# Global attention of a fused four-layer kernel: two query tiles per turn, V as the stationary operand, sums spread by a product

## Reference

```python
def _L2_conv_ref(x, cfc, theta_w, theta_b, phi_w, phi_b, g_w, g_b, out_w, out_b):
    ...
    gate = jax.nn.sigmoid(z)[:, :, None]
    s = xf * gate
    theta = jnp.einsum('oc,ncl->nol', theta_w, s) + theta_b[None, :, None]
    phi = jnp.einsum('oc,ncl->nol', phi_w, s) + phi_b[None, :, None]
    g = jnp.einsum('oc,ncl->nol', g_w, s) + g_b[None, :, None]
    attn = jax.nn.softmax(jnp.einsum('nci,ncj->nij', theta, phi), axis=-1)
    nl = jnp.einsum('ncj,nij->nci', g, attn)
    nl = jnp.einsum('oc,ncl->nol', out_w, nl) + out_b[None, :, None]
    out = s + nl
```

## Time and profile before

| | us |
|---|---|
| median of 3 runs (7589.86 to 7595.02) | 7592.06 |
| the profiled execution | 7591.81 |
| its span in the trace | 7590.1 |
| `softmax2` of batch 0, from the first copy of a query tile to the last write of `nl` | 1067.6 to 1517.2 |
| `softmax2` of batch 1 | 1576.5 to 2026.2 |

### The profile page before, as it was taken

How to read it: one execution, slowest core, us unless ns; L and a number is a source line. 1 busy time by engine, 2 the same in 40 slices (tenths; PEclk the granted TensorE clock), 3 DMA queues, 4 the chain that set the end, 5 groups by cost and what they waited for, 6 DMA issues and landing times. The chain is left out here.

```text
span 7590.1 us, 146447 instructions
## 1 busy us (share of the span) xinstructions
PE 6756.7 (89%) x42848; PEld 4634.2 (61%) x42848; DVE 6281.8 (83%) x9625; ACT 5783.1 (76%) x9094; POOL 5374.7 (71%) x3396
## 2 busy tenths in 40 slices
PE   6777889989779999999999999999999999999998
PEld 4656457767546666666666666666666666666666
DVE  4333754444459999999999999999999999999997
ACT  4454112222259999999999999999999999999997
POOL 3333000000049999999999999999999999999997
PEclk9988999999989999999999999999999999999998
DMA  2000000000010000000000000000000000000000
GB/s 71 20 22 22 1 1 0 0 0 0 10 52 10 1 1 1 1 1 2 10 1 1 1 1 1 2 27 1 1 1 1 1 2 2 4 4 4 4 4 6
DMA packets 75943, 56.06 MB, mean 7 GB/s; under 512 B 50776, under 2 KB 73464, under 8 KB 75032
## 3 DMA queue, kind: packets, MB, share of 16 engines
q1 hardware_dynamic: 72512, 53.88, 2.5%
q10 hardware_dynamic: 3288, 0.33, 0.0%
HBM read 37.80 MB, written 16.37 MB: 7 GB/s over the span
## 5 line engine op out<-in xcount | busy, mean ns | idle before, releaser
L1524 POOL TENSOR_TENSOR a_s<-a_s,a_v 128x784 f32<-128x784 f32 x1568 | 2912.8, 1858 | 321.6 <-ACT a_s L1735 305.7
L1560 PE MATMUL a_right_sides<-a_s,diag_d 128*128 128x392 f32 x6272 | 2294.0, 509 | 9.1 <-POOL a_s L1524 1.0
L1560 PEld LDWEIGHTS a_right_sides<-a_s,diag_d 128*128 128x128 f32 x6272 | 1136.7, 191 | 1057.5 <-POOL a_s L1524 306.7
L1656 DVE SCALAR_TENSOR_TENSOR a_kan<-a_s,spline_c,a_kan 128x784 f32<-128x784 f32 x1568 | 1622.9, 1035 | 51.6 <-issue 0.6
L1583 PEld LDWEIGHTS a_weighed<-a_V,a_probT 112*128 112x128 f32 x10976 | 1374.7, 193 | 162.2
L1517 POOL TENSOR_TENSOR a_inner<-a_inner,a_x 128x784 f32<-128x784 f32 x784 | 1458.6, 1860 | 0.0
L1583 PE MATMUL a_weighed<-a_V,a_probT 112*128 112x65 f32 x10976 | 1365.5, 270 | 0.0
L1735 ACT ACTIVATE a_s<-a_v 128x784 f32<-128x784 f32 x1568 | 1335.0, 852 | 4.7
L1726 ACT ACTIVATE a_v<-a_a 128x784 f32<-128x784 f32 x1568 | 1335.9, 852 | 0.3
L1572 PE MATMUL a_turned<-ident,a_prob 128*112 128x128 f32 x5488 | 856.7, 279 | 228.4 <-ACT a_probT L1742 226.6
L1627 DVE TENSOR_SCALAR a_x<-a_scores 128x392 f32<-128x392 f32 x1568 | 877.7, 560 | 20.1 <-PE a_scores L1547 20.1
(11 more groups left out here) (192 smaller groups left out, 6842.1 us busy)
## 6 DMA issues: line engine op xcount, KB each, us to landing
rows<-bias_rows_dram SPq DMA_DIRECT2D x112, 91.0 KB
X<-in_x_dram SPq DMA_DIRECT2D x4, 1568.0 KB, 13.7
a_q<-q_dram SPq DMA_DIRECT2D x392, 16.0 KB, 2.0
mask<-in_window_mask_dram SPq DMA_DIRECT2D x56, 98.0 KB
v_dram<-V SPq DMA_DIRECT2D x14, 227.5 KB, 2.3
a_V<-v_dram SPq DMA_DIRECT2D x4, 796.2 KB
q_dram<-Q SPq DMA_DIRECT2D x14, 224.0 KB, 1.9
k_dram<-K SPq DMA_DIRECT2D x14, 224.0 KB, 1.9
```

Of the source, the lines that this page charges most:

```text
L1524: eng.tensor_tensor(s, s, v, ALU.mult).then_inc(cubed, 1)
L1560: mm = eng.matmul(up[:, j, 0:SUB], steps[i][:, :], cubes[g][:, SUB * j:SUB * (j + 1)], start=(i == 0), stop=(i == 1))
L1656: eng.scalar_tensor_tensor(F, banked((s1, s2)[j][g][:, :]), c[:, 3 + j:4 + j], F, ALU.mult, ALU.add).then_inc(left_added, 1)
```

## The change

`softmax2` takes the queries in 14 pairs of tiles (`PAIR` = 224 queries, turn u) instead of 28 tiles. The scores of the two tiles (h = 0, 1) come one after the other, as eight groups. A chunk is now two key tiles of both query tiles, [112, 2, 224]: the same number of elements as before, 14 chunks per pair. In the products that weigh the values the operands change places: `gT` of a key tile is stationary, and the 224 turned columns move, so the output has channels on partitions and needs no turning. The division changes with it: DVE multiplies the identity by the inverse sums (`share`), PE multiplies that with a matrix of ones, which gives the inverse sums in every channel's row, and DVE copies them (`spread`) and multiplies the output with them into `nl` (`keep_spread`). ACT copies the even chunks and so the first of each pair, DVE the odd ones. ACT no longer places the output. The addition of `s` to the stream moves from DVE in `project_out2` to POOL in `project2`.

```diff
-                project2(nc, m, b, s, theta, phi, gT, gate_scale, gate_bias)
+                project2(nc, m, b, theta, phi, gT, gate_scale, gate_bias)
...
+            @block.gpsimd
+            def _(pool):
+                pool.wait_ge(gated, HALVES)
+                for f in range(HALVES):
+                    X = m.X[:, HALVES * b + f, :]
+                    pool.tensor_tensor(X, X, s[:, f, :], ALU.add).then_inc(with_s, 1)
+                pool.wait_ge(with_s, HALVES)
...
+        probT = [sb(f"probT{r}", [TILE, 2, PAIR]) for r in range(2)]
+        tp = [ps(f"turned{i}", [TILE, 2, 256]) for i in range(2)]
+        op = [ps(f"op{r}", [P, 2, 256]) for r in range(2)]
...
+        def copied(c, u):
+            return (copied_v if c % 2 else copied_a, 7 * (u + 1) + c // 2 + 1)
+
+        def copy_chunk(eng, copy, u, c, done):
+            eng.wait_ge(turned, 14 * u + c + 29)
+            eng.wait_ge(pv_done, 14 * u + c + 13)
+            copy(probT[c % 2][:, :, :], tp[c % 2][:, :, 0:PAIR]).then_inc(done, 1)
...
+                def values(eng, u, r):
+                    eng.wait_ge(exp_done, 2 * (u + 1))
+                    for c in range(TILES // 2 + 1):
+                        if c < TILES // 2:
+                            eng.wait_ge(*(copied(c - 2, u) if c >= 2 else copied(c + 12, u - 1)))
+                            for j in range(2):
+                                at = TILE * (2 * c + j)
+                                for h in range(2):
+                                    mm = eng.transpose(tp[c % 2][:, j, TILE * h:TILE * (h + 1)], prob[r][h][:, at:at + TILE], m.ident[0:TILE, 0:TILE])
                             mm.then_inc(turned, 1)
                         if c == 1:
-                            eng.wait_ge(o_normed, t + 1)
+                            eng.wait_ge(o_placed, u + 1)
                         if c >= 1:
-                            eng.wait_ge(*copied(c - 1, t))
-                            for j in range(4):
-                                k = 4 * (c - 1) + j
-                                mm = eng.matmul(op[:, :], probT[(r + c - 1) % 2][:, j, :], gT[:, k, :], start=(k == 0), stop=(k == TILES - 1))
+                            eng.wait_ge(*copied(c - 1, u))
+                            for j in range(2):
+                                k = 2 * (c - 1) + j
+                                mm = eng.matmul(op[r][:, 0, 0:PAIR], gT[:, k, :], probT[(c - 1) % 2][:, j, :], start=(k == 0), stop=(k == TILES - 1))
                             mm.then_inc(pv_done, 1)
...
+                def spread_shares(eng, u, r):
+                    eng.wait_ge(share_made, 2 * (u + 1))
+                    for h in range(2):
+                        mm = eng.matmul(op[r][:, 1, TILE * h:TILE * (h + 1)], ones[:, :], share[r][:, h, :], start=True, stop=True)
+                    mm.then_inc(shares_spread, 1)
...
-                pipeline(pe, TILES, [(scores, 0), (turn_out, 2), (values, 1)])
+                pipeline(pe, TURNS, [(scores, 0), (spread_shares, 2), (values, 1)])
...
-                pipeline(dve, TILES, [(row_max, 0), (normalise, 1)])
+                pipeline(dve, TURNS, [(row_max, 0), (keep_spread, 2), (normalise, 1)])
...
-                pipeline(act, TILES, [(copies, 1), (place_out, 2), (exponent, 0)])
+                pipeline(act, TURNS, [(copies, 1), (exponent, 0)])
...
-                for f in range(HALVES):
-                    X = m.X[:, HALVES * b + f, :]
-                    dve.tensor_tensor(X, X, s[:, f, :], ALU.add).then_inc(with_s, 1)
```

More of the change, by code:

```diff
@@ L1122, in copied @@
[L1122 to L1132, removed]
+        q = [sb(f"q{r}", [P, PAIR]) for r in range(2)]
@@ new lines, in softmax2 @@
+        prob = [[sb(f"prob{r}{h}", [TILE, L]) for h in range(2)] for r in range(2)]
+        probT = [sb(f"probT{r}", [TILE, 2, PAIR]) for r in range(2)]
+        share = [sb(f"share{r}", [TILE, 2, TILE]) for r in range(2)]
+        ones = sb("ones", [TILE, P])
+        spread = sb("spread", [P, PAIR])
+        gmax = [sb(f"gmax{r}", [TILE, 2, 4]) for r in range(2)]
+        rmax = [sb(f"rmax{r}", [TILE, 2]) for r in range(2)]
+        nmax = [sb(f"nmax{r}", [TILE, 2]) for r in range(2)]
+        rsum = [sb(f"rsum{r}", [TILE, 2]) for r in range(2)]
@@ L1142, in _ @@
+                pipeline(pool, TURNS, [(stage_q, 0)])
             @block.tensor
             def _(pe):
[L1144 to L1158, removed]
-                            for j in range(4):
-                                at = TILE * (4 * c + j)
-                                mm = eng.transpose(tp[(r + c) % 2][:, j, :], prob[r][:, at:at + TILE], m.ident[0:TILE, 0:TILE])
+                def scores(eng, u, r):
+                    eng.wait_ge(q_ready, u + 1)
+                    for h in range(2):
+                        for g in range(4):
+                            eng.wait_ge(s_copied, 8 * u + 4 * h + g + 1)
+                            for j in range(2):
+                                at = SUB2 * (2 * g + j)
+                                mm = eng.matmul(scp[g % 2][:, j, 0:SUB2], q[r][:, TILE * h:TILE * (h + 1)], phi[:, at:at + SUB2], start=True, stop=True)
+                            mm.then_inc(s_made, 1)
@@ L1183, in _ @@
+                pe.sem_inc(s_made, 16)
+                pe.sem_inc(turned, 28)
+                pe.sem_inc(pv_done, 14)
+                pe.wait_ge(ones_set, 1)
+                pipeline(pe, TURNS, [(scores, 0), (spread_shares, 2), (values, 1)])
             @block.vector
             def _(dve):
[L1185 to L1194, removed]
@@ L1208, in _ @@
-                pipeline(dve, TILES, [(row_max, 0), (normalise, 1)])
+                dve.sem_inc(copied_v, 7)
+                dve.sem_inc(o_placed, 2)
+                pipeline(dve, TURNS, [(row_max, 0), (keep_spread, 2), (normalise, 1)])
+                dve.wait_ge(o_placed, TURNS + 2)
             @block.scalar
             def _(act):
[L1212 to L1225, removed]
-                pipeline(act, TILES, [(copies, 1), (place_out, 2), (exponent, 0)])
-                act.wait_ge(o_placed, TILES + 1)
-def project_out2(nc, m, b, s, nl):
+                def copies(eng, u, r):
+                    for c in range(0, TILES // 2, 2):
+                        copy_chunk(eng, eng.copy, u, c, copied_a)
@@ new lines, in exponent, with project_out2 @@
+                def exponent(eng, u, r):
+                    for h in range(2):
+                        eng.wait_ge(max_ready, 2 * u + h + 1)
+                        eng.activation(prob[r][h][:, :], prob[r][h][:, :], ACT.Exp, bias=nmax[r][:, h:h + 1], accum_out=rsum[r][:, h:h + 1]).then_inc(exp_done, 1)
+                act.sem_inc(copied_a, 7)
+                pipeline(act, TURNS, [(copies, 1), (exponent, 0)])
+                act.wait_ge(exp_done, 2 * TURNS)
+def project_out2(nc, m, b, nl):
```

68 lines of the change are left out of this document (30 added, 38 removed).

## The result

The changed kernel takes 7478.99 us (median of four, 7471.93 to 7492.06) against 7590.96 (7589.22 to 7595.02): ratio 0.9858, interval 0.9845 to 0.987. A second comparison gave 7476.05 against 7587.33: 0.9851, 0.9836 to 0.9867.

What follows compares the result with a forecast made beforehand. PE and what makes it wait bound `softmax2`. Pairs gain 97.2 us, batch ends lose 9.6, `project_out2` gains 3.8: 91.4 off 7591.81 gives 7500.4, with the median 0.25 above, so 7501; range 7484 to 7541.

Steps and rivals of the forecast that it cites:

- Step 1: Weighing products in `softmax2`: 56 passes of 224 columns at 0.19 us replace 112 of 128, gaining 1.57 us per pair.
- Step 2: First copies of a pair: PE waits 0.58 us for chunk 0 and 0.35 for chunk 1, gaining 2.11 per pair.
- Step 3: Chunks between first and last: copies just fit behind PE's work, 1.145 us a chunk, cover 0.09, no further gain.
- copies bind: Rival on step 3's chunks: slower copies or handing over lengthen each chunk, 7512 to 7546, likely 7525; chance 0.17.
- Steps 4 to 6: Per pair: last copy gains 0.06 us, product with the ones loses 0.19, scores in eight groups lose 0.08.
- Step 7: Batch ends: PE waits 3.6 us for the last exponentials, then a lower clock; net loss 4.8 a batch, 9.6 altogether.
- Step 8: `project_out2` without DVE's additions ends one piece behind PE, at 13.2 us: gain 1.9 a batch, 3.8 in all.
- Step 9: POOL's additions in `project2`: 7.4 us for each half, 14.9 for both, hidden, costing nothing.
- the rest unnamed: Outcomes outside the forecast and named rivals, spread over both sides; no cause or size given.

## Why the prediction was wrong

It was right in the layer that it worked out, and wrong in what it left out.

- **The sum for the layer** was 91.4; the layer gave 96.8. A pair was to take 28.45 and took 28.23. `softmax2` gave 4.9 more than forecast and `project_out2` 1.4 more, while `project2` lost 0.8 in these traces.
- **Step 1**, the pass of 224 columns at 0.19: (1.156 - 0.385) / 4 = 0.193. Over 1568 passes that is 4 us less gain than forecast. That it is columns that count was shown with 256 of them. Width itself earns nothing: two tiles now move 224 columns per key tile and pass where they moved 2 x 128.
- **Step 2**, the first copies: right in mechanism, 1.24 instead of 1.35 for chunk 0 and a stand of 0.10 instead of 0.35 for chunk 1. From the copy's end to PE's product 0.05 passed, where I had 0.15, and DVE began the spread 1.08 after the transpose, not 1.23; the two instructions took 0.39 each (I had 0.43 and 0.40). This is worth 0.36 a pair more than forecast. The 0.15 went wrong by the operand and not by the engine. In the old order the copied tile is the stationary operand and has to be loaded after the copy: with ACT's copy too, the copy ends at 1284.73, the load starts at 1284.84, the product at 1284.87. In the new order the copied tile moves, and with DVE's copy first (1296.68 + 0.61) PE starts 0.07 behind it.
- **Step 3**: chunks held at 1.156; the thin cover was enough, and the rival "copies bind" did not come.
- **Steps 4 to 6**: 0.29 for the last copy (0.30 forecast), the product with the ones 0.43 (0.39 forecast), the scores 10.57 from their start to that product (1299.40 to 1309.97), which is 32 passes of 0.330 without a visible loss; the 10.74 in the row includes the last pass's own length.
- **Step 7**: PE waited 3.07 us beyond the product (3.6 forecast), then ran at half its clock as forecast, for 6.8 us in batch 0 and 3.4 in batch 1 (3.7 forecast).
- **Step 8**: 1.9 a batch was right for batch 1 (17.5 to 15.7). In batch 0 the clock stayed up, PE took 10.76 instead of 12.42, and the stage gained 3.4. The mechanism was named, but I took both batches alike. What keeps the clock up in one batch and not in the other, behind the same 2.53 us of rest, was not found.
- **Step 9**: POOL took 6.82 an addition (7.4 forecast) and stayed hidden: `project2` took 42.1 against 42.0.

**The step that failed** is none of the nine, but the sentence behind them: that the profiled execution goes to 7500.4 when the layer's sum is taken off, with all else unchanged. The sum put the change of the untouched last attention at nothing, without a reason; it measured 16.8. The kernel before has 16 to 17 us in that layer that most other kernels here don't have: of seven pauses tried on it one left 13 of them, and among the edits of the changed kernel the one with the addition on DVE has 20. 7501 less 16.8 is 7484, and 5 us more from the layer give 7479, the measured median. That it fits to the microsecond is partly luck, for the medians of the kernel before alone lie between 7587.3 and 7592.1 here. The layer's 5 us alone would have left the time at 7496, inside the range. The rivals did not hold this case either; "the rest unnamed" took its place. What remains open is why just these moments are bad. The trace shows what happens (PE's clock halves for 6.8 us in single blocks) and that two executions of one kernel repeat the layer's time to 0.1 us, though their first parts differ by 5 us. The blocks need not be the same ones: the first long one was the 81st in one execution of the kernel before and the 79th in the other. What in PE's work sets it off was not found.

## What to carry to other kernels

Price an operation by moving columns and ask which operand has fewer per product: here 112 queries against 128 channels. Before reordering the mathematics, look who makes the first copy of a loop and what stands ahead of it on that engine: a swap of two engines alone gave 54 us where the whole change gave 97, and undoing it in the changed kernel cost 41. And cut both traces at the borders of the layer that was changed: here a layer that was not touched moved by 17 us one way and 20 the other, and then a median credits or blames the wrong edit.

## What the runs showed of the hardware

An untouched layer of 5.53 ms took 5529 to 5550 us in different kernels, through short halvings of PE's clock in blocks that keep PE busy for 25 of 27.3 us. Each of three kernels traced twice repeated its time within 0.3 us, and in one program the length of a pause in front of the layer changed it by 11.5 us. A pause of 1344 columns in front of it made the whole kernel 11 us faster. From the end of a copy to the product that uses it, 0.14 to 0.15 us passed where the copied tile was the stationary operand, and 0.05 to 0.07 where it moved.
